# A batched bilinear interaction on one core: half-size mix units, and a table for the order of TensorE's units

## The reference, cut to what matters

```python
# feature: r_feature, (512, 200, 64) f32; weight: (200, 64, 64) f32
B, F, E = (256, 200, 64)   # B of the data is 512
bilinear = jnp.einsum('bie,ied->bid', feature, weight)
out = jnp.einsum('bid,bjd->bij', bilinear, feature)   # (512, 200, 200)
```

## Time and profile before

| | us |
|---|---|
| median of three executions (lowest, highest) | 310.88 (308.45, 311.99) |
| the profiled execution, its own time | 306.8 |
| its span, first to last instruction | 305.0 |
| mean granted TensorE clock in it | 0.961 of full speed |

### The profile page before, as it was taken

One profiled execution on the slowest core, in us unless ns is written; L12 is line 12 of the kernel. 1 busy time (PEld: TensorE's weight loads), 2 busy tenths in 40 slices (PEclk: granted clock), 3 DMA queues, 4 the chain that ended last, 5 costly groups with the idle time before them and its releaser, 6 DMA issues.

```text
span 305.0 us, 14640 instructions
## 1 busy us (share of the span) xinstructions
PE 243.2 (80%) x6800; PEld 210.9 (69%) x6800; DVE 152.8 (50%) x180; ACT 130.1 (43%) x181; POOL 12.5 (4%) x23
## 2 busy tenths in 40 slices
PE   6839849999877586999867785898985774998990
PEld 2437749888776476878866675866885674996970
DVE  0153634556755443537644454634765554775621
ACT  2153515445544324245444243542653451665420
POOL 2004800000000000000000000000000000000000
PEclk9996997999999979899999799999999999999997
DMA  7999997999999999968999999986999999599995
GB/s 219 415 417 357 363 410 302 324 376 373 369 360 416 407 419 420 409 280 354 374 366 408 383 411 417 388 355 248 389 371 391 408 387 417 210 402 381 409 408 218
DMA packets 22172, 112.35 MB, mean 368 GB/s; under 512 B 4320, under 2 KB 4320, under 8 KB 21856
## 3 DMA queue, kind: packets, MB, share of 16 engines
q1 hardware_dynamic: 22112, 111.43, 92.6%
HBM read 29.49 MB, written 81.92 MB: 365 GB/s over the span
## 4 chain that ended last, share of the span: by engine, by line
PE 76%; issue 16%; DMA 2%; SPq 2%; DVE 1%; ACT 1%
PE psum L322 50%; PE psum L285 17%; PE psum L339 8%; DMA w_sb<-w_dram 2%; SPq L166 2%; PE psum L305 1%; DVE tile L355 1%; ACT mixed L376 0%; ACT w_sb L390 0%; SPq L178 0%
## 5 line engine op out<-in xcount | busy, mean ns | idle before, releaser
L322 PE MATMUL psum<-x_sb,mixed 64*64 64x200 f32 x3072 | 163.1, 351 | 14.0 <-issue 12.5
L322 PEld LDWEIGHTS psum<-x_sb,mixed 64*64 64x64 f32 x3072 | 133.3, 139 | 27.9 <-issue 17.9
L355 DVE COPY tile<-psum 128x800 f32<-128x800 f32 x100 | 99.2, 992 | 88.6 <-PE psum L322 79.8
L355 ACT COPY tile<-psum 128x800 f32<-128x800 f32 x100 | 82.4, 826 | 70.2 <-PE psum L322 54.0
L285 PE MATMUL psum<-x_sb,w_sb 64*64 64x64 f32 x3072 | 64.4, 221 | 35.1 <-issue 34.2
L285 PEld LDWEIGHTS psum<-x_sb,w_sb 64*64 64x64 f32 x3072 | 61.7, 134 | 40.5 <-issue 37.7
L376 ACT COPY mixed<-psum 64x512 f32<-64x512 f32 x48 | 27.8, 580 | 43.2 <-PE psum L285 42.6
L376 DVE COPY mixed<-psum 64x512 f32<-64x512 f32 x48 | 33.1, 689 | 16.7 <-PE psum L285 15.5
L378 ACT COPY mixed<-psum 128x512 f32<-128x512 f32 x24 | 14.1, 586 | 36.3 <-PE psum L285 36.2
L378 DVE COPY mixed<-psum 128x512 f32<-128x512 f32 x24 | 16.6, 691 | 22.3 <-PE psum L285 22.2
L339 PE MATMUL psum<-x_sb,tails 128*32 128x200 f32 x512 | 25.0, 342 | 0.1
(11 more groups left out here) (5 smaller groups left out, 1.7 us busy)
## 6 DMA issues: line engine op xcount, KB each, us to landing
out_dram<-tile SPq DMA_DIRECT2D x192, 400.0 KB, 5.6
x_sb<-x_dram SPq DMA_DIRECT2D x64, 400.0 KB, 6.9
out_tail_dram<-tile SPq DMA_DIRECT2D x8, 400.0 KB, 4.2
w_sb<-w_dram SPq DMA_DIRECT2D x1, 1152.0 KB, 15.2
w_sb<-w_dram SPq DMA_DIRECT2D x4, 256.0 KB, 7.3
w_sb<-w_dram SPq DMA_DIRECT2D x1, 1024.0 KB, 13.1
```

Of the source, the lines that this page charges most:

```text
L322: last = nc.tensor.matmul(psum[half_rows(pair), n % BANK_PAIRS * 2 + h, a * FIELDS:(a + 1) * FIELDS], mixed[half_rows(h), (CHUNKS * g + c) ...
L355: copy(tile[:, k % SLOTS, engine], psum[:, bank:bank + 2, 0:2 * FIELDS]).then_inc(copied[engine], 1)
```

## The change

Mix units are cut in half: 8 fields, 4 to each bank, 64 instructions; 8 of them make a chunk, 96 the kernel. Their copies take 256 columns instead of 512, and there are twice as many. The order of the units is no longer worked out from MIX_AFTER and its like but read from a table, ORDER, with one string for each chunk of each group: s is a score unit, m a mix unit of the next chunk, t a tail unit, x the tail mix. Loads and crosswise copies of the weights keep their size, by a constant of their own (W_FIELDS = 16). The mix unit that crosses into part 1 of x is now the fifth of eight (CROSSING), and which pieces of part 1 the scores wait for, and which that mix unit, is worked out from the table (WAITED = 2, 3, 2, 2). All else stands as it was. The diff, cut at the places that only rename the constant for the weights:

```diff
--- before.py
+++ after.py
@@ -27,20 +27,26 @@
 BANK = 512
 BANK_PAIRS = 4
-BANK_FIELDS = BANK // HALF_SAMPLES
+BANK_FIELDS = BANK // HALF_SAMPLES // 2
 MIX_FIELDS = 2 * BANK_FIELDS
 MIX_UNITS = CHUNK // MIX_FIELDS
 TILES = QUADS // 4
-MIX_AFTER = (1, 3, 5, 6)
-TAIL_MIX_AFTER = 6
-LAST_WAITED = MIX_AFTER[(PART - CHUNK) // MIX_FIELDS]
-TAIL_CHUNK = [1] * (GROUPS - 1) + [CHUNKS - 1]
-TAIL_AFTER = [(2, 4)] * (GROUPS - 1) + [(5, 7)]
+ORDER = (
+    ("ssmsmsmssmssmsssmsmsmxsss", "ssmsssmssmstmtmsmsmsssmsss", "ssmsmsssmsmsmsmssmssmsss"),
+    ("ssmssmssmsmssmxsmssmsmsss", "msstmsssmsmstsmsmsssmsmsss", "mssssssmssmsmsmsmsmssmss"),
+    ("msmsssmsmsssmsmsssmsmssxs", "ssmsmtssmtmsmsssssmssmsmss", "mssssmssmsmsmsssmsmssmss"),
+    ("ssmsmsssmsmsmsmsmssssmxss", "sssmssmsssmssmsmsmsmsmss", "sssssssssssstsssst"),
+)
+PIECE_TILES = PIECE_QUADS // 4
+CROSSING = (PART - CHUNK) // MIX_FIELDS
+WAITED = [-(-"".join(order[0].split("m")[:CROSSING + 1]).count("s") // (2 * PIECE_TILES)) for order in ORDER]
 SLOTS = 6
 WARM_UPS = 8
@@ -50,16 +56,17 @@
+W_FIELDS = 16
 W_OWN = FIELDS // 2
-OWN_FIELDS = MIX_FIELDS // 2
-W_CUTS = [OWN_FIELDS * n for n in range(MIX_UNITS)] + [CHUNK // 2, CHUNK, W_OWN]
+OWN_FIELDS = W_FIELDS // 2
+W_UNITS = CHUNK // W_FIELDS
+W_CUTS = [OWN_FIELDS * n for n in range(W_UNITS)] + [CHUNK // 2, CHUNK, W_OWN]
 def own_index(field):
-    unit, r = divmod(field, MIX_FIELDS)
-    own = min(MIX_FIELDS, FIELDS - unit * MIX_FIELDS) // 2
+    unit, r = divmod(field, W_FIELDS)
+    own = min(W_FIELDS, FIELDS - unit * W_FIELDS) // 2
     return r // own, unit * OWN_FIELDS + r % own
@@ -80,20 +87,20 @@
         n += 1
     for g in range(GROUPS):
         for c in range(CHUNKS):
-            for t in range(TILES):
-                for u in range(2):
-                    score(n, g, c, t, u)
-                    n += 1
-                if c == TAIL_CHUNK[g] and t in TAIL_AFTER[g]:
-                    tail(n, g, TAIL_AFTER[g].index(t))
-                    n += 1
-                to, chunk = next_chunk(g, c)
-                if t in MIX_AFTER and to < GROUPS:
-                    mix(n, to, chunk, MIX_AFTER.index(t))
-                    n += 1
-                if c == 0 and t == TAIL_MIX_AFTER:
+            to, chunk = next_chunk(g, c)
+            done = {"s": 0, "m": 0, "t": 0, "x": 0}
+            for kind in ORDER[g][c]:
+                k = done[kind]
+                done[kind] += 1
+                if kind == "s":
+                    score(n, g, c, k // 2, k % 2)
+                elif kind == "m":
+                    mix(n, to, chunk, k)
+                elif kind == "t":
+                    tail(n, g, k)
+                else:
                     tail_mix(n, g)
-                    n += 1
+                n += 1
 def count_copies():
...
@@ -264,16 +271,18 @@
                 first = c * CHUNK + m * MIX_FIELDS
                 if c == 0 and m == 0:
                     wait_part0(g)
-                if g == 0 and c == 0:
-                    pe.wait_ge(w_loaded[m], 16)
+                w_unit, later = divmod(m * MIX_FIELDS, W_FIELDS)
+                if g == 0 and c == 0 and not later:
+                    pe.wait_ge(w_loaded[w_unit], 16)
                     for e in range(2):
-                        pe.wait_ge(w_crossed[e], m + 1)
-                elif g == 0:
-                    pe.wait_ge(w_crossed[2], 2 * ((c - 1) * MIX_UNITS + m + 1 + (c > 1)))
-                if first <= PART < first + MIX_FIELDS:
-                    for p in range(4 * LAST_WAITED // PIECE_QUADS + 1, PIECES):
+                        pe.wait_ge(w_crossed[e], w_unit + 1)
+                elif g == 0 and not later:
+                    pe.wait_ge(w_crossed[2], 2 * ((c - 1) * W_UNITS + w_unit + 1 + (c > 1)))
+                if m == CROSSING and c == 1:
+                    for p in range(WAITED[g], PIECES):
                         wait_part1(g, p)
                 bank = n % BANK_PAIRS * 2
                 for r in range(BANK_FIELDS):
@@ -299,7 +308,7 @@
                 wait_bank(n, 0)
                 if g == 0:
-                    pe.wait_ge(w_crossed[2], 2 * (MIX_UNITS + 1))
+                    pe.wait_ge(w_crossed[2], 2 * (W_UNITS + 1))
                 for r in range(TAIL):
                     for h in range(HALVES):
                         last = nc.tensor.matmul(
@@ -311,8 +320,8 @@
             def score(n, g, c, t, u):
                 if t == 0 and u == 0:
                     wait_copies(NUMBER["mix", g, c, MIX_UNITS - 1])
-                if c == 0 and u == 0 and t <= LAST_WAITED and 4 * t % PIECE_QUADS == 0:
-                    wait_part1(g, 4 * t // PIECE_QUADS)
+                if c == 0 and u == 0 and t % PIECE_TILES == 0 and t // PIECE_TILES < WAITED[g]:
+                    wait_part1(g, t // PIECE_TILES)
                 for a in range(2):
                     quad = 4 * t + 2 * u + a
                     for pair in range(2):
@@ -367,7 +376,7 @@
             def mix(n, g, c, m):
                 eng.wait_ge(unit_ready, n + 1)
                 swap = (m + engine) % 2
-                source = psum[:, n % BANK_PAIRS * 2 + swap, :].rearrange(
+                source = psum[:, n % BANK_PAIRS * 2 + swap, 0:BANK_FIELDS * HALF_SAMPLES].rearrange(
                     "p (r q s) -> p q r s", r=BANK_FIELDS, q=QUADS)
                 first = m * MIX_FIELDS + swap * BANK_FIELDS
                 to = mixed[:, (CHUNKS * g + c) % 2, :, first:first + BANK_FIELDS, :]
@@ -384,7 +393,7 @@
                     "p (r q b) -> p q b r", r=TAIL, q=QUADS)
                 copy(tails[half_rows(engine), :, 0:4:3, engine, :], source).then_inc(copied[engine], 1)
-            for n in range(MIX_UNITS):
+            for n in range(W_UNITS):
                 own = slice(n * OWN_FIELDS, (n + 1) * OWN_FIELDS)
                 eng.wait_ge(w_loaded[n], 16)
                 copy(w_sb[half_rows(engine), 1, own, :], w_sb[half_rows(1 - engine), 0, own, :]).then_inc(
```

More of the change, by code:

```diff
@@ L183, in _ @@
                 load_part0(sp, 0, n)
-            for n in range(1, MIX_UNITS):
+            for n in range(1, W_UNITS):
                 load_w(n)
@@ L187, in _ @@
                 load_part1(sp, 0, n)
-            for n in range(MIX_UNITS, len(W_CUTS) - 1):
+            for n in range(W_UNITS, len(W_CUTS) - 1):
                 load_w(n)
@@ L218, in _ @@
             done = 0
-            units = list(range(MIX_UNITS, CHUNKS * MIX_UNITS))
-            for unit in units[:MIX_UNITS] + [CHUNKS * MIX_UNITS] + units[MIX_UNITS:]:
+            units = list(range(W_UNITS, CHUNKS * W_UNITS))
+            for unit in units[:W_UNITS] + [CHUNKS * W_UNITS] + units[W_UNITS:]:
                 own = slice(unit * OWN_FIELDS, min((unit + 1) * OWN_FIELDS, W_OWN))
-                pool.wait_ge(w_loaded[MIX_UNITS if unit < 2 * MIX_UNITS else MIX_UNITS + 1], 16)
+                pool.wait_ge(w_loaded[W_UNITS if unit < 2 * W_UNITS else W_UNITS + 1], 16)
                 for h in range(HALVES):
```

## The result

| | kernel before | changed kernel |
|---|---|---|
| median of 20 executions each (lowest, highest), us | 309.97 (307.01, 312.11) | 309.27 (306.93, 311.57) |
| ratio (executions as below) | 1 | 1.0081 (95%: 1.0048 to 1.0114) |
| profiled execution, span, us | 305.0 | 306.2 |
| median, a second comparison on one chip | 308.17 | 308.30, ratio 1.0056 (1.0015 to 1.0098) |
| a third comparison | 308.63 | 308.78, ratio 1.0043 (0.9990 to 1.0095) |

The ratios leave out every execution more than 1.5% above the fastest of its kernel, which in the second comparison takes 9 of 29 from the kernel before and none of 12 from the changed one, and further down takes away one execution of 570.7 us and one of 377.6 us.

What follows compares the result with a forecast made beforehand. TensorE was taken to wait at every 256th instruction for packets delayed by data on the DMA engines. Terms +0.5 - 2.3 - 2.0 - 1.5 + 1.2 - 0.4 = -4.5 us gave 306.3 us, from 310.88; range 300 to 315.

Steps and rivals of the forecast that it cites:

- What bounds the kernel: TensorE waits at every 256th instruction for a 16 KB packet through busy DMA engines; a block costs the longer of work and fetch.
- Semaphore instructions: At bank wait L240, 48 more mix units add 0 to 48 semaphore instructions to the blocks: +0.5 us, at most +1.0.
- Even blocks: In chunk 1 of groups 2 and 3, evening out blocks takes back 2.3 of 3.8 us idle.
- The lead at a block's end: Blocks ending in scores let the next fetch be asked for 0.84 us earlier, in about five stretches: -2.0 us, at best 4.2.
- Blocks that begin with mix: Some 20 waiting blocks that would newly begin with mix save 0.15 us each: -1.5 us taken, bounds 0 and 6.0.
- Copies: Twice as many, smaller mix copies cost +1.2 us (bounds 0 and +5); shorter last copies ahead of the first score give -0.4.
- Earlier needs: The mix crossing into x's second part stands up to half a block earlier in chunk 0; late loads mostly covered: 0 us.
- no difference: Rival, chance 0.28: TensorE's gains in chunks 0 and 2 return as longer fetches, chunk 1's matmuls stay; 310 to 312 us.
- its first mechanism: In chunks 0 and 2 data and fetch are coupled, so TensorE's gain returns as longer fetch; in chunk 1 the matmuls stay.
- its second: Semaphore instructions shift the blocks, so a table right early may have blocks start in scores later; same 310 to 312 us.
- Slower: Rival, chance 0.25: scores at a block's end queue stores ahead of the next packet, up to 0.4 us a block, +12 us.
- The last sign: Sign of being right, in TensorE's waits: those ahead of mixes are many and those ahead of scores few.

Runs made afterwards that it cites:

- The shifted table: Changed kernel with 16 more tiny warm-up matmuls, moving every block boundary 64 instructions earlier in the table; 308.20 us against 308.30 for the changed kernel.
- the wide kernel: Kernel before with each mix call working on two neighbouring fields (128 columns), 3072 fewer instructions, same data; 297.1 us against 309.83, ratio 0.9612.

## Why the prediction was wrong

- **What bounds the kernel**: right. Nearly all waits still lie 256 instructions apart, or a multiple of that, the instruction queue still has 53 packets, and the issue waits fall by 22.4 us, to 24.3, when data is taken away. The rule of the Trainium skill that I had set against the trace ("Runtime: NRT & Kernel Launch", Instruction fetch mechanics: crossing a block's boundary is mostly hidden) would have given about the time measured, but by a mechanism that doesn't fit the 39 waits, 46.4 us.
- **Semaphore instructions, +0.5**: 0. The bank wait has 41 in place of 42.
- **Even blocks, -2.3**: did not come. Chunk 1 of group 2 has 26.50 - 24.21 = 2.3 us idle, as before, that of group 3 2.6, not 1.4, and those of groups 0 and 1 now have 3.5 and 2.2. I had priced idle time in chunk 1 as something that a table can take back, but that idle time is the same fetch floor, and it moves.
- **The lead at a block's end, -2.0**: failed. The shifted table, with about 20 blocks the wrong way round and 8 the right way, against 4 and about 30, is at most 0.5 us slower. I had let an unmeasured lead of up to 64 instructions into the sum at half its bound; no run shows one worth a microsecond.
- **Blocks that begin with mix, -1.5**: failed, by the same run. The 0.15 us a block came from two blocks of each kind, in chunks with different histories. The three blocks shown above take 5.37, 5.93 and 5.35 us, rows 5 have 5.10 to 6.40.
- **Copies, +1.2 - 0.4**: the cover held. Matmuls waited 1.9 us for copies (1.0, 0.5, and 0.4 for a tile), 1.3 before, and weight loads about 3.4 us in place of 3.3, so the +1.2 was too much; the wait ahead of the first score is 1.0 in place of 1.3. The wait for GpSimd's weights, 1.6 us, was not in my list at all, though the first m of the first string stands there to be read; taking it away gained nothing.
- **Earlier needs, 0**: the second profiled execution of the changed kernel did wait 3.0 us for x at the crossing mix of group 1, the first did not. Its time, 310.0 us, is 1.7 us above the median of its comparison; what the wait cost wasn't taken apart.
- **The rivals**: the time is that of "no difference", and its first mechanism holds, not its second: the table does shift the blocks as it says. Its own number, 310 to 312, was slightly high. It had the right argument in one sentence, that what TensorE gains comes back as a longer fetch, and I gave it 0.28. "Slower" by stores queued ahead of the fetch by 0.15 us a block or more would have had the shifted table ahead of the table by over 4 us; it is ahead by 0.1, and at most by 1.8.

Of the signs that I had named, issue time fell from 48.9 to 46.4 us (44.7 and 46.1 in the two later profiled executions) and not to 40, chunk 1 of groups 2 and 3 kept over 1 us idle, and the waits ahead of scores grew from 8 to 17. The last sign was badly chosen: in the timeline shown the wait falls two matmuls short of the mix unit, so it is listed under scores although the block begins with mix.

Taken together: three terms failed, -2.3, -2.0 and -1.5, -5.8 us in all. They are all gains in the placing of work around a floor that the placing hardly touches: the packets of waiting blocks still start 3.2 us after the preceding block began (median), and the 2.5 us by which issue time fell came back in waits for x, GpSimd's weights and copies. What is left of my sum without them is +1.3 us; measured was no difference within 0.2% (0.6 us) by the means, so the +0.5 for semaphores and the +1.2 for copies aren't borne out either.

## What to carry to other kernels

When waits stand at multiples of 256 instructions of an engine and there are as many instruction packets as blocks of 256, count the blocks: in this kernel each costs about the longer of its work and its fetch. By that account reordering can help only while some blocks have more work than a fetch takes and others less; here the order was already even, and only fewer instructions, or less data beside the fetch, shortened the time. Before pricing what a wait costs, ask what the next limit is: here taking away 48 us of waits gave 12 us, part of it from less work, because waits for data and for output slots stood right behind.

## What the runs showed of the hardware

- One-column f32 calls with a 64x64 weight, four in a row with the same input and output partitions, added 85 us to TensorE's busy time for 3072 instructions, 28 ns each, where a mix unit has 10.6 ns an instruction. The calls of mix and score alternate between partition halves and these don't; whether that is the reason was not tested.
- 768 mix calls with 128 columns take 53.6 us of busy time, 1536 with 64 columns 64.4 (line of the wide kernel, then of the kernel before). That is 70 and 42 ns a call: the second 64 columns add 28 ns, so by this estimate some 14 of the 42 ns belong to the call and 28 to its columns.

```profile
L289 PE MATMUL psum<-x_sb,w_sb 64*64 64x128 f32 x1536 | 53.6, 273 | 9.4 <-POOL w_sb L227 4.1
```

```profile
L285 PE MATMUL psum<-x_sb,w_sb 64*64 64x64 f32 x3072 | 64.4, 221 | 35.1 <-issue 34.2
```

- The instruction packets take 0.95 us each in the median under the data load of this kernel, and a waiting block begins 1.4 us after its packet's end (1.1 to 1.6 us in the kernel before).
